# Row maxima of attention scores taken three rounds later, and their bf16 split moved inside GpSimd's turn

## The chip, the cores and the metric

The kernel runs on one core of one Trainium2 chip. The metric is the device time of one execution in microseconds (us), the median over several executions. It covers one transformer layer for 32 sequences of 256 tokens with 128 features.

## What is computed

The reference, cut to what matters:

```python
qkv = x @ W_qkv.T + b_qkv                      # x: (32, 256, 128), 16 heads of size 8
att = einsum('bthd,bshd->bhts', q, k) / sqrt(8)
att_v = einsum('bhts,bshd->bthd', softmax(att), v)
x = layernorm(x + att_v @ W_out.T + b_out)
# mixture of experts, 8 experts of 128 x 128, the 2 best per token, and one shared expert
x = layernorm(x + moe(x))
```

The change concerns the softmax only: exp(score - maximum of the row) is computed by putting the negated row maxima into the score matmul as two more rows of its contraction (a high and a low bf16 part), so the maxima of a batch must be known before its scores are exponentiated.

## The kernel before, in words

The engines are TensorE (PE in the profile), VectorE (DVE), ScalarE (ACT), GpSimd (POOL) and SyncE (SP, which issues DMAs). Each has its own instruction list, written out by hand, and waits on semaphores. Each list is in order.

The kernel has two stages. **Attention** takes the first 438 us or so, **the experts** the rest (groups of 512 tokens, lines 883 and 1141). The attention stage is a software pipeline over the 32 sequences, called batches. One step of the pipeline is a **turn** (a `Slot`, line 186, run from s = -4 to 31 by `slots`, line 207). In turn s each engine works on several batches at once:

- `proj`, batch s+4: q and k projections (PE L777 and L794), copied out by ACT (L616, L624), split into three bf16 parts by POOL (L466 to L495) and sent to HBM by SP (L355, L362)
- `stack`, batch s+3: SP reads the parts back as stacks of rows (L330), PE makes v (L790)
- `maxi`, batch s+2: PE computes plain scores into PSUM (`row_maxima_scores`, L699), DVE reduces each to row maxima (L1014)
- `neg`, batch s+1: POOL splits the negated maxima into two bf16 parts (L444, L446), PE transposes them (L826), DVE copies them out (L1055), SP writes them into the q stack (L336)
- `soft`, batch s: PE computes shifted scores (`shifted_scores`, L686), ACT takes exp (L561), PE multiplies by v (L714)
- `tail`, `norm`, `gated` (batches s-1, s-2, s-3): normalization of the attention result (PE L810, L848; DVE L1048, L1064), output projection (PE L770), residual (`x_bo`, POOL L460; `res`, DVE L1026) and layernorm (DVE L1029 to L1036; POOL `rstd` L473 and `x1_new` L482; PE transpose L842), transposed copy kept by POOL (L433), gate logits (PE L817)

PE's turn has eight **rounds** p = 0 to 7 of two heads each, that is 16 **steps**, one head per step. For a step PE issues, alternately, two matmuls L686 of batch s and two matmuls L699 of batch s+2; they use different halves of the rows of the array (`other = 1 - h % 2`, line 697) and overlap. Between rounds stand the other matmuls: L770 and L777 after round 0, L790 and L794 after round 2 (`PE_VQ`), L810, L817 and L826 after round 4 (`PE_TOK`), L842 and L848 after round 6 (`PE_BACK`), and L714 after rounds 1, 3, 5 and 7.

DVE's turn has the 16 reductions L1014 in order of the steps, and between them: `res` (L1026) after step 1's, stats (L1029) after step 2's, aggregate and `var_eps` (L1032, L1036) after step 4's, and after step 9's the copies and products L1048, L1055, L1058, L1064. `res` waits for PE's L777 of the same turn (L1020), the group after step 9 waits for L826 (L1044). In turn 30 the first routing work of the expert stage (`biased_scores`, L961 to L963) stands on DVE ahead of step 5.

**The banks.** Three PSUM banks hold scores for the maxima. PE may write a step's scores only when DVE has reduced the step that used the bank before:

```python
if i == 0 and (b.later(1) or h >= MAX_BACK[h]):
    pe.wait_ge(max_red, b.count(H, h + 1 - MAX_BACK[h]))
```

`three_banks(twice)` (line 157) gives the bank of each of the 16 heads and, as `MAX_BACK`, how many steps back the same bank was used. Sixteen heads don't divide by three, so one place of the order is irregular: banks run 0, 1, 2, 0, 1, 2, ... and at that place 0, 1, 2, 1. The distance is 3 everywhere but there, where it is 2, 4, 2, 4 for four heads in a row. ACT's banks (`EXP_BANK`) have the same rule with their own place.

Of the kernel before, what the change touches and what calls it, by code (L numbers as in the profile page):

```python
# [7 lines left out]
ALU = mybir.AluOpType  # L8
# [41 lines left out]
def attention_moe_layer(nc, x, xT, wqT, wkT, wvT, bq, bk, bv, woT, bo, gateT, ebias, rank, w1T, w3T, w2T, out):  # L50
# [3 lines left out]
    NT = T // P  # L54
    D = 8
    H = C // D
# [10 lines left out]
    PAIRS = H // 2  # L67
    assert C == P and H == 16 and NT == 2 and ROWS + 2 <= HALF

    with ExitStack() as ctx:  # L70
        def sb(name, shape, dt=F32):
            return ctx.enter_context(nc.sbuf_tensor(name, shape, dt))

        def sem(name):
            return ctx.enter_context(nc.semaphore(name))
# [20 lines left out]
        minus_half, ones = sb("minus_half", [P, GT]), sb("ones", [P, NT, 2, PAIRS])  # L96
# [10 lines left out]
        negmax = [sb(f"negmax{r}", [P, NT, H]) for r in range(2)]  # L107
# [3 lines left out]
        max_two = [sb(f"max_two{r}", [P, NT, 2, 2, PAIRS], BF16) for r in range(2)]  # L111
# [13 lines left out]
        max_ps, score_ps, av_ps, misc = banks[0:3], banks[3:6], banks[6], banks[7]  # L125
# [18 lines left out]
        v_set = sem("v_set")  # L144
        max_mm, max_red = sem("max_mm"), sem("max_red")
        max_hi_set, max_lo_set, max_T, max_rows_set = sem("max_hi_set"), sem("max_lo_set"), sem("max_T"), sem("max_rows_set")
# [10 lines left out]
        def three_banks(twice):  # L157

            order = [0, 1, 2] * (twice // 3) + [0, 1, 2, 1] + [0, 1, 2] * (4 - twice // 3)
            return order, [next(d for d in range(1, H) if order[(h - d) % H] == order[h]) for h in range(H)]  # L160

        MAX_BANK, MAX_BACK = three_banks(3)
        EXP_BANK, EXP_BACK = three_banks(9)


# [19 lines left out]

        class Slot:
            def __init__(self, i, s):
                self.load, self.proj, self.stack, self.maxi, self.neg, self.soft, self.tail, self.norm, self.gated = (
                    Batch(i, s + k, B) for k in (5, 4, 3, 2, 1, 0, -1, -2, -3))

        PE_YK, PE_VQ, PE_TOK, PE_BACK = 0, 2, 4, 6
        DVE_RES, DVE_STATS, DVE_AGGR, DVE_TOK = 1, 2, 4, 9
        ACT_K, ACT_ATT, ACT_V, ACT_Q, ACT_ATTC, ACT_X1T = 2, 4, 5, 6, 13, 14
# [209 lines left out]
        def _(pool):  # L405
# [27 lines left out]
                    pool.tensor_copy(x1T[:, bass.ds(b.n * T, T)], x1T_new[:]).then_inc(x1T_kept, 1)  # L433

            def rows_and_parts(t):
                b = t.neg
                if b.live:

                    negated = negmax[b.ring % 2][:].rearrange("p i (u g) -> p i u g", u=2)
                    two = max_two[b.ring % 2]  # L440
                    pool.wait_ge(max_red, b.count(H, H))
                    if b.later(2):
                        pool.wait_ge(max_T, b.count(1, -1))
                    pool.tensor_tensor(two[:, :, :, 0, :], negated, ones[:], ALU.mult).then_inc(max_hi_set, 1)  # L444
                    pool.wait_ge(max_hi_set, b.count(1, 1))
                    pool.tensor_tensor(two[:, :, :, 1, :], negated, two[:, :, :, 0, :], ALU.subtract).then_inc(max_lo_set, 1)  # L446
                p, o = t.proj, t.tail
                k_split, q_split = k_parts[p.ring % 2], q_parts[p.ring % 2]
                if o.live:
# [19 lines left out]
                b = t.norm  # L469
# [7 lines left out]
                        pool.wait_ge(x1_kept, b.count(16, 0))  # L477
                if p.live:
                    pool.tensor_tensor(k_split[:, 1, :], kf[:], k_split[:, 0, :], ALU.subtract).then_inc(split_step, 1)
                if b.live:  # L480
                    for i in range(NT):
                        pool.tensor_scalar(x1_new[:, i, :], res[:, i, :], mv[:, i, 0:1], rstd[:, i:i + 1],  # L482
                                           ALU.subtract, ALU.mult).then_inc(x1_set, 1)
# [194 lines left out]
        def _(pe):  # L678
# [12 lines left out]
            def row_maxima_scores(b, h, i):  # L691

                if i == 0 and h == 0:
                    pe.wait_ge(stack_in[b.ring], b.lap(64, 64))
                if i == 0 and (b.later(1) or h >= MAX_BACK[h]):
                    pe.wait_ge(max_red, b.count(H, h + 1 - MAX_BACK[h]))
                other = 1 - h % 2
                first, last = HALF * other, HALF * other + ROWS
                mm = pe.matmul(max_ps[MAX_BANK[h]][:, i * T:(i + 1) * T], q_stack[b.ring][first:last, h // 2, i * P:(i + 1) * P],  # L699
                               k_stack[b.ring][first:last, h // 2, :], start=True, stop=True)  # L700
                if i == NT - 1:
                    mm.then_inc(max_mm, 1)
# [37 lines left out]
            def slot(t, first=0, last=PAIRS):  # L740
                for p in range(first, last):
                    if (t.soft.c, p) == (B - 1, PE_ROUTED):
                        pe.wait_ge(max_red, H * B)
                        routing_by_tile(max_ps[2], 0, CHUNKS - 1, 1)
                    for h in (2 * p, 2 * p + 1):
                        for n in range(NT):
                            if t.soft.live:
                                shifted_scores(t.soft, h, n)
                            if t.maxi.live:
                                row_maxima_scores(t.maxi, h, n)  # L750

                    b = t.norm
                    if p == PE_YK and (b.live or t.proj.live):

                        if b.live:
                            pe.wait_ge(attc_set, b.count(1, 1))
                        elif t.soft.live:
                            pe.wait_ge(max_rows_set, t.soft.count(1, 1))
                        if t.gated.live:
                            pe.wait_ge(x1T_set, t.gated.count(1, 1))  # L760
                        if not b.live and t.proj.later(1):
                            pe.wait_ge(qk_f, t.proj.count(2, 0))
                            if t.proj.later(2):
                                pe.wait_ge(v_set, t.maxi.count(2, 2))
                    if b.live and p == PE_YK:

                        if b.c == 0:
# [4 lines left out]
                    b = t.proj  # L772
# [11 lines left out]
                    b = t.stack  # L784
# [7 lines left out]
                    b = t.proj  # L792
# [10 lines left out]
                    b = t.tail  # L803
# [8 lines left out]
                    b = t.gated  # L812
# [6 lines left out]
                    b = t.neg  # L819
# [17 lines left out]
                    b = t.norm  # L837
# [6 lines left out]
                    b = t.tail  # L844
# [66 lines left out]
        def _(dve):  # L911
# [26 lines left out]
            step = [0]  # L938
# [50 lines left out]
            def slot(t, first=0, last=H):  # L989
                for h in range(first, last):  # L990
# [14 lines left out]
                        dve.wait_ge(res_set, t.norm.count(1, 1))  # L1005
                    if t.norm.live and h == DVE_AGGR:
                        dve.wait_ge(stats_set, t.norm.count(NT, NT))
                    b = t.maxi
                    if b.live:
                        dve.wait_ge(max_mm, b.count(H, h + 1))  # L1010
                        if h == 0 and b.later(2):
                            dve.wait_ge(max_lo_set, b.count(1, -1))
                        column = PAIRS * (1 - h % 2) + h // 2
                        nc.vector.tensor_reduce(negmax[b.ring % 2][:, :, column], max_ps[MAX_BANK[h]][:].rearrange("p (i s) -> p i s", i=NT),  # L1014
                                                AX_X, ALU.max, negate=True).then_inc(max_red, 1)
                    b = t.norm
                    if b.live and h == DVE_RES:
# [27 lines left out]
                    b = t.tail  # L1045
# [3 lines left out]
                    b = t.neg  # L1049
# [6 lines left out]
                    b = t.gated  # L1056
                    if b.live and h == DVE_TOK:
                        nc.vector.tensor_copy(logits[:, bass.ds(b.n * NT, NT), :], gate_ps).then_inc(logits_set, 1)  # L1058
                    b = t.tail
# [166 lines left out]
```

## Time and profile before

| what | us |
|---|---|
| median of 3 runs | 787.43 (787.11 to 788.23) |
| the profiled execution, its own time | 788.83 |
| its span, from first to last instruction | 786.7 |
| PE busy | 750.0 (95% of the span) |
| DVE busy | 645.2 (82%) |
| ACT busy | 512.5 (65%) |
| POOL busy | 479.0 (61%) |

All times of the trace are counted from the start of the span. The busy time of an engine is an average over two stages with different limits: over the expert stage DVE is busy about two thirds of the time, in the attention stage nearly always. The attention stage must therefore be read by itself. A matmul's record lasts longer than the time until the next one starts, since matmuls are pipelined.

### The profile page before, as it was taken

How to read it: one execution, taken by the hardware profiler on the slowest of the kernel's cores; microseconds unless marked ns; L12 is line 12 of the kernel's file. 1: busy time of each engine (PE TensorE's matmuls, PEld its weight loads, DVE VectorE, ACT ScalarE, POOL GpSimd, SP SyncE). 2: the span in 40 equal slices, each digit the busy share in tenths (PEclk: the TensorE clock that was granted, in tenths of full speed). 3: DMA queues.
4: the chain of work that ended last, by engine and by line, in shares of the span. 5: the costliest groups of instructions: out<-in, count | busy, mean ns of one | idle time of the engine just before them, and what ended most of it. 6: DMA issues, size and time to landing. Idle time of an engine off the chain costs nothing.

```text
span 786.7 us, 20507 instructions
## 1 busy us (share of the span) xinstructions
PE 750.0 (95%) x6948; PEld 525.1 (67%) x6948; DVE 645.2 (82%) x1386; ACT 512.5 (65%) x1037; POOL 479.0 (61%) x653
## 2 busy tenths in 40 slices
PE   2889999999999999999999999899999999999995
PEld 1345555555555555555554688788888888888885
DVE  7689899999999999999998547976776666666665
ACT  1158788888888888888889645445545444554542
POOL 4345587876767667676634465565565566555554
PEclk9999999999999999999999999999999999999998
DMA  4646766566656665565531654454555545565440
GB/s 116 174 116 165 213 175 182 147 164 178 153 158 163 173 170 154 157 162 166 151 82 36 180 127 106 104 144 123 130 124 129 129 129 127 124 131 124 121 97 27
DMA packets 201449, 108.84 MB, mean 138 GB/s; under 512 B 10392, under 2 KB 200984, under 8 KB 201368
## 3 DMA queue, kind: packets, MB, share of 16 engines
q1 hardware_dynamic: 200048, 105.88, 52.1%
q10 hardware_dynamic: 1320, 1.91, 1.1%
q8 instruction: 47, 0.77, 0.5%
q14 instruction: 34, 0.28, 0.1%
HBM read 73.41 MB, written 33.82 MB: 136 GB/s over the span
## 4 chain that ended last, share of the span: by engine, by line
PE 86%; DVE 6%; DMA 3%; issue 2%; SPq 2%; ACT 1%; POOL 0%; POOLq 0%; DVEq 0%; ACTq 0%
PE bank L879 15%; PE bank L714 15%; PE bank L686 10%; PE bank L721 8%; PE bank L722 8%; PE bank L723 8%; PE bank L699 7%; PE bank L790 2%; PE bank L770 2%; PE bank L810 2%; DVE negmax L1014 2%; PE bank L777 2%; PE bank L794 2%; PE bank L817 1%; DMA q_stack<-max_rows 1%
## 5 line engine op out<-in xcount | busy, mean ns | idle before, releaser
L1014 DVE TENSOR_REDUCE negmax<-bank 128x2 f32<-128x512 f32 x512 | 320.1, 679 | 15.2 <-PE bank L699 12.8
L561 ACT ACTIVATE probs<-bank 128x512 f32<-128x512 f32 x512 | 291.8, 606 | 60.8 <-PE bank L686 57.0
L665 ACT ACTIVATE q_stack<-k_stack 128x512 f32<-128x512 f32 x128 | 80.8, 631 | 154.9 <-DVE k_stack L1077 154.9
L699 PE MATMUL bank<-k_stack,q_stack 48*128 48x256 bf16 x1024 | 162.7, 282 | 13.9 <-DMA k_stack<-k_parts_dram 9.8
L686 PE MATMUL bank<-q_stack,k_stack 50*128 50x256 bf16 x1024 | 156.2, 274 | 4.2 <-DMA q_stack<-max_rows 2.1
L1077 DVE TENSOR_TENSOR k_stack<-bank,probs 128x512 f32<-128x512 f32 x128 | 88.3, 690 | 74.8 <-PE bank L723 74.4
L714 PE MATMUL bank<-probs,v_aug 128*32 128x256 f32 x2048 | 137.1, 385 | 0.4 <-ACT attT L572 0.4
L686 PEld LDWEIGHTS bank<-q_stack,k_stack 50*128 50x128 bf16 x1024 | 75.2, 95 | 87.6 <-ACT probs L561 44.4
L721 PE MATMUL bank<-x_hi,hi_w 128*128 128x512 f32 x288 | 126.5, 439 | 3.1 <-DVE k_stack L1087 1.2
L722 PE MATMUL bank<-x_hi,lo_w 128*128 128x512 f32 x288 | 114.0, 396 | 0.0
L723 PE MATMUL bank<-x_lo,hi_w 128*128 128x512 f32 x288 | 113.6, 394 | 0.0
L514 POOL TENSOR_TENSOR k_stack<-k_stack,probs 128x512 f32<-128x512 f32 x48 | 62.0, 1291 | 50.9 <-DVE k_stack L1087 42.2
L699 PEld LDWEIGHTS bank<-k_stack,q_stack 48*128 48x128 bf16 x1024 | 71.4, 96 | 32.0 <-issue 14.3
L879 PEld LDWEIGHTS bank<-w_sb,k_stack 128*128 128x128 f32 x640 | 83.4, 191 | 7.1
L714 PEld LDWEIGHTS bank<-probs,v_aug 128*32 128x32 f32 x2048 | 53.6, 109 | 49.2 <-issue 15.2
L879 PE MATMUL bank<-w_sb,k_stack 128*128 128x128 f32 x640 | 84.0, 274 | 0.0
L514 POOL TENSOR_TENSOR place<-k_stack,probs 128x512 f32<-128x512 f32 x48 | 61.9, 1290 | 30.4 <-PE bank L879 25.6
L649 ACT ACTIVATE probs<-probs 128x512 f32<-128x512 f32 x128 | 78.9, 616 | 0.4 <-DMA probs<-route_dram 0.4
L514 POOL TENSOR_TENSOR k_stack<-q_stack,probs 128x512 f32<-128x512 f32 x32 | 41.1, 1284 | 53.0 <-DVE q_stack L1087 44.1
L1087 DVE TENSOR_TENSOR k_stack<-bank,q_stack 128x512 f32<-128x512 f32 x96 | 65.6, 683 | 4.1 <-POOL k_stack L514 3.6
L723 PEld LDWEIGHTS bank<-x_lo,hi_w 128*128 128x128 f32 x288 | 54.1, 188 | 13.4
L721 PEld LDWEIGHTS bank<-x_hi,hi_w 128*128 128x128 f32 x288 | 54.5, 189 | 11.4 <-DVE k_stack L1087 1.6
(103 smaller groups left out, 1111.3 us busy)
## 6 DMA issues: line engine op xcount, KB each, us to landing
probs<-route_dram SPq DMA_DIRECT2D x128, 256.0 KB, 4.9
q_stack<-q_parts_dram SPq DMA_DIRECT2D x64, 192.0 KB, 3.3
k_stack<-k_parts_dram SPq DMA_DIRECT2D x64, 192.0 KB, 4.1
k_parts_dram<-k_parts SPq DMA_DIRECT2D x32, 192.0 KB, 2.2
q_parts_dram<-q_parts SPq DMA_DIRECT2D x32, 192.0 KB, 2.1
xT_sb<-xT SPq DMA_DIRECT2D x32, 128.0 KB, 2.3
k_parts_dram<-k_parts SPq DMA_DIRECT2D x32, 128.0 KB, 2.0
q_parts_dram<-q_parts SPq DMA_DIRECT2D x32, 128.0 KB, 1.9
```

Of the source, the lines that this page charges most:

```text
L514: pool.tensor_tensor(hid_s[n % DEPTH], hid[n % DEPTH], weight2_b[n - 1], ALU.mult).then_inc(hids_set, 1)
L561: nc.scalar.activation(probs[h][:], score_ps[EXP_BANK[h]][:].rearrange("p (j t) -> p j t", j=NT), ACT.Exp).then_inc(exp_done, 1)
L665: nc.scalar.activation(act[n % DEPTH], gated[n % DEPTH] if n else up1_ps[0][:], ACT.Silu).then_inc(act_set, 1)
L686: mm = pe.matmul(score_ps[EXP_BANK[h]][:, j * T:(j + 1) * T], k_stack[b.ring][first:last, h // 2, j * P:(j + 1) * P], q_stack[b.ring][firs ...
L699: mm = pe.matmul(max_ps[MAX_BANK[h]][:, i * T:(i + 1) * T], q_stack[b.ring][first:last, h // 2, i * P:(i + 1) * P], k_stack[b.ring][first: ...
L714: mm = pe.matmul(av_ps[32 * hh:32 * hh + 32, half * T:(half + 1) * T], v_aug[b.ring][:, 2 * j + half, u, hh, :], probs[4 * quad + hh][:, j ...
L721: pe.matmul(ps[:], w_hi[m][:, n, :], hi[:], start=start, stop=False)
L722: pe.matmul(ps[:], w_lo[m][:, n, :], hi[:], start=False, stop=False)
L723: return pe.matmul(ps[:], w_hi[m][:, n, :], lo[:], start=False, stop=stop)
L879: mm = pe.matmul(down_ps[r][:, i * P:(i + 1) * P], (hid_s if n else hid)[n % DEPTH][:, i * P:(i + 1) * P], w2_sb[:, n, :], start=(n == 0 a ...
L1014: nc.vector.tensor_reduce(negmax[b.ring % 2][:, :, column], max_ps[MAX_BANK[h]][:].rearrange("p (i s) -> p i s", i=NT), AX_X, ALU.max, neg ...
L1077: nc.vector.tensor_tensor(gated[n % DEPTH], up1_ps[n % DEPTH][:], weight_b[e], ALU.mult).then_inc(gated_set, 1)
```

## The change

It has four parts:

1. A turn's 16 steps of maxima no longer belong to one batch. Steps 0 to 5 work on heads 10 to 15 of batch s+1 (`neg`), steps 6 to 15 on heads 0 to 9 of batch s+2 (`next`, the new name of `maxi`). This holds on PE and on DVE alike. `maxima(step)` gives batch and head.
2. The bank order of the maxima is `three_banks(12)` in place of `three_banks(3)`. Banks go with heads, not with steps.
3. POOL's split of the maxima (L444, L446) moves from the start of its turn to behind the second k part (L479), ahead of `x1_new` (L482). It still waits until all 16 heads of the batch are reduced (in the block marked "..." ahead of `b = t.norm` stand the removed lines, unchanged).
4. The wait of L764 and DVE's waits name the new objects; the counts follow from batch and head.

Nothing else moves: the number of instructions of every kind, the transposes, the copies and the DMAs of the maxima keep their places in the turn.

```diff
-        MAX_BANK, MAX_BACK = three_banks(3)
+        MAX_BANK, MAX_BACK = three_banks(12)
...
-                self.load, self.proj, self.stack, self.maxi, self.neg, self.soft, ...
+                self.load, self.proj, self.stack, self.next, self.neg, self.soft, ...
+            def maxima(self, step):
+                return (self.neg, step + H - MAX_FROM) if step < MAX_FROM else (self.next, step - MAX_FROM)
+        MAX_FROM = 6
...
             def rows_and_parts(t):
-                b = t.neg
-                if b.live:
-                    negated = negmax[b.ring % 2][:].rearrange("p i (u g) -> p i u g", u=2)
-                    two = max_two[b.ring % 2]
-                    pool.wait_ge(max_red, b.count(H, H))
-                    if b.later(2):
-                        pool.wait_ge(max_T, b.count(1, -1))
-                    pool.tensor_tensor(two[:, :, :, 0, :], negated, ones[:], ALU.mult).then_inc(max_hi_set, 1)
-                    pool.wait_ge(max_hi_set, b.count(1, 1))
-                    pool.tensor_tensor(two[:, :, :, 1, :], negated, two[:, :, :, 0, :], ALU.subtract).then_inc(max_lo_set, 1)
...
                 if p.live:
                     pool.tensor_tensor(k_split[:, 1, :], kf[:], k_split[:, 0, :], ALU.subtract).then_inc(split_step, 1)
+                b = t.neg
+                if b.live:
...
+                b = t.norm
                 if b.live:
                     for i in range(NT):
                         pool.tensor_scalar(x1_new[:, i, :], res[:, i, :], mv[:, i, 0:1], rstd[:, i:i + 1],
...
                     for h in (2 * p, 2 * p + 1):
+                        ahead, head = t.maxima(h)
                         for n in range(NT):
                             if t.soft.live:
                                 shifted_scores(t.soft, h, n)
-                            if t.maxi.live:
-                                row_maxima_scores(t.maxi, h, n)
+                            if ahead.live:
+                                row_maxima_scores(ahead, head, n)
...
-                                pe.wait_ge(v_set, t.maxi.count(2, 2))
+                                pe.wait_ge(v_set, t.next.count(2, 2))
...
-                    b = t.maxi
+                    b, head = t.maxima(h)
                     if b.live:
-                        dve.wait_ge(max_mm, b.count(H, h + 1))
-                        if h == 0 and b.later(2):
+                        dve.wait_ge(max_mm, b.count(H, head + 1))
+                        if head == 0 and b.later(2):
                             dve.wait_ge(max_lo_set, b.count(1, -1))
-                        column = PAIRS * (1 - h % 2) + h // 2
-                        nc.vector.tensor_reduce(negmax[b.ring % 2][:, :, column], max_ps[MAX_BANK[h]][:].rearrange("p (i s) -> p i s", i=NT),
+                        column = PAIRS * (1 - head % 2) + head // 2
+                        nc.vector.tensor_reduce(negmax[b.ring % 2][:, :, column], max_ps[MAX_BANK[head]][:].rearrange("p (i s) -> p i s", i=NT),
                                                 AX_X, ALU.max, negate=True).then_inc(max_red, 1)
```

## Rows read from the trace of the kernel before

**Rows 1.** The page's costliest group: the reductions (busy, mean ns; idle before, releaser)

```profile
L1014 DVE TENSOR_REDUCE negmax<-bank 128x2 f32<-128x512 f32 x512 | 320.1, 679 | 15.2 <-PE bank L699 12.8
```

**Rows 2.** Busy time by stretch (stretch, length, PE, PEld, DVE, ACT, POOL, PEclk, DMA share, GB/s)

```profile
120.00:243.00 123.00, 122.85 (x1536) 70.97 (x1536) 120.10 (x260) 106.75 (x235) 89.32 (x155) 1.00 0.62 163
243.00:366.00 123.00, 123.00 (x1544) 71.06 (x1540) 120.22 (x261) 105.74 (x231) 85.58 (x150) 1.00 0.61 163
```

**Rows 3.** Waits between 60 and 440 us (us in total, times, longest us)

```profile
DVE negmax L1014 <- PE bank L699: 3.1, 6, 1.8
...
PEld bank L699 <- DVE negmax L1014: 1.9, 3, 1.3
```

**Rows 4.** Timeline of DVE, turn 16 (start us, us, engine line op, xcount)

```profile
245.30 0.42 DVE L1026 TENSOR_TENSOR res<-bank,x_bo 128x256 f32<-128x256 f32 x1
...
246.76 1.27 DVE L1014 TENSOR_REDUCE negmax<-bank 128x2 f32<-128x512 f32 x2
...
248.57 3.09 DVE L1014 TENSOR_REDUCE negmax<-bank 128x2 f32<-128x512 f32 x5
251.80 0.36 DVE L1048 RECIPROCAL recip_sum<-bank 128x32 f32<-128x32 f32 x1
...
252.62 5.00 DVE L1014 TENSOR_REDUCE negmax<-bank 128x2 f32<-128x512 f32 x8
257.60 0.42 DVE L1026 TENSOR_TENSOR res<-bank,x_bo 128x256 f32<-128x256 f32 x1
```

**Rows 5.** Timeline of PE, the same turn

```profile
244.66 0.60 PE L777 MATMUL bank<-xT_sb,wk_sb 128*128 128x256 f32 x2
...
246.86 0.38 PE L699 MATMUL bank<-k_stack,q_stack 48*128 48x256 bf16 x2
...
248.48 0.38 PE L699 MATMUL bank<-k_stack,q_stack 48*128 48x256 bf16 x2
...
251.38 0.29 PE L826 MATMUL bank<-ident_bf,max_two 128*32 128x128 bf16 x2
...
253.69 0.44 PE L842 MATMUL bank<-ident,x_new 128*128 128x128 f32 x2
...
256.96 0.60 PE L777 MATMUL bank<-xT_sb,wk_sb 128*128 128x256 f32 x2
```

**Rows 6.** Timeline of POOL, the same turn and the start of the next

```profile
249.53 0.68 POOL L479 TENSOR_TENSOR k_parts<-kf,k_parts 128x256 bf16<-128x256 f32 x1
...
256.69 0.25 POOL L446 TENSOR_TENSOR max_two<-negmax,max_two 128x32 bf16<-128x32 f32 x1
```

**Rows 7.** Timeline of PE, then of DVE, turn 29, rounds 2 and 3

```profile
406.20 0.37 PE L686 MATMUL bank<-q_stack,k_stack 50*128 50x256 bf16 x2
407.57 0.28 PE L699 MATMUL bank<-k_stack,q_stack 48*128 48x256 bf16 x1 [0.99 <-DVE negmax L1014]
...
406.24 1.27 DVE L1014 TENSOR_REDUCE negmax<-bank 128x2 f32<-128x512 f32 x2
```

**Rows 8.** Timeline of DVE, turn 30

```profile
416.16 0.43 DVE L1026 TENSOR_TENSOR res<-bank,x_bo 128x256 f32<-128x256 f32 x1 [0.66 <-PE bank L770]
...
417.93 2.55 DVE L962 RECIPROCAL q_stack<-q_stack 128x384 f32<-128x384 f32 x1
...
421.82 0.36 DVE L1048 RECIPROCAL recip_sum<-bank 128x32 f32<-128x32 f32 x1 [0.75 <-PE bank L826]
```

**Rows 9.** Timeline of DVE, then of PE, turns -2 to 0

```profile
21.94 1.29 DVE L1014 TENSOR_REDUCE negmax<-bank 128x2 f32<-128x512 f32 x2 [3.58 <-PE bank L699]
...
27.51 7.47 DVE L1014 TENSOR_REDUCE negmax<-bank 128x2 f32<-128x512 f32 x12 [1.45 <-PE bank L699]
...
39.51 2.68 DVE L1014 TENSOR_REDUCE negmax<-bank 128x2 f32<-128x512 f32 x4 [1.45 <-PE bank L699]
42.10 0.27 DVE L1055 COPY max_rows<-bank 32x256 bf16<-32x256 bf16 x1
...
45.20 0.39 PE L686 MATMUL bank<-q_stack,k_stack 50*128 50x256 bf16 x1 [0.37 <-DMA q_stack<-max_rows]
```

More of the change, by code:

```diff
@@ L187, in __init__ @@
             def __init__(self, i, s):
-                self.load, self.proj, self.stack, self.maxi, self.neg, self.soft, self.tail, self.norm, self.gated = (
+                self.load, self.proj, self.stack, self.next, self.neg, self.soft, self.tail, self.norm, self.gated = (
                     Batch(i, s + k, B) for k in (5, 4, 3, 2, 1, 0, -1, -2, -3))
+            def maxima(self, step):
+                return (self.neg, step + H - MAX_FROM) if step < MAX_FROM else (self.next, step - MAX_FROM)
+        MAX_FROM = 6
         PE_YK, PE_VQ, PE_TOK, PE_BACK = 0, 2, 4, 6
@@ L479, in rows_and_parts @@
                     pool.tensor_tensor(k_split[:, 1, :], kf[:], k_split[:, 0, :], ALU.subtract).then_inc(split_step, 1)
+                b = t.neg
+                if b.live:
+                    negated = negmax[b.ring % 2][:].rearrange("p i (u g) -> p i u g", u=2)
+                    two = max_two[b.ring % 2]
+                    pool.wait_ge(max_red, b.count(H, H))
+                    if b.later(2):
+                        pool.wait_ge(max_T, b.count(1, -1))
+                    pool.tensor_tensor(two[:, :, :, 0, :], negated, ones[:], ALU.mult).then_inc(max_hi_set, 1)
+                    pool.wait_ge(max_hi_set, b.count(1, 1))
+                    pool.tensor_tensor(two[:, :, :, 1, :], negated, two[:, :, :, 0, :], ALU.subtract).then_inc(max_lo_set, 1)
+                b = t.norm
                 if b.live:
```

## The prediction

> **What bounds the kernel now.** The busy shares of the whole span mix two stages, so I read the attention stage by stretch first. Between 120 and 366 us PE is busy in 245.85 of 246 us and DVE in 240.3, that is 12.0 us of each 12.3 us turn; ACT with 212.5 us and POOL with 174.9 have room [rows 2]. PE is the bound and DVE stands 0.3 us per turn behind it. The waits say the same: from 60 to 440 us PE's weight loads waited for a reduction three times, 1.9 us together, and DVE waited for score matmuls six times, 3.1 us [rows 3]. The three banks between the two engines work almost without a stall.
>
> Then the timeline of turn 16, engine by engine. PE's L777 starts at 244.66 and again at 256.96: a turn is 12.30 us [rows 5]. DVE is tied to PE at two places. `res` starts at 245.30, just after L777 ends at 244.66 + 0.60 = 245.26; the reciprocal after step 9 starts at 251.80, 0.13 after L826 ends at 251.67 [rows 4, 5]. From the reciprocal to the next `res` DVE needs 5.80 us without a gap, PE from the end of L826 to the end of L777 5.89. So neither half of the turn has more than some 0.2 us to give, and what holds PE up in the first half moves L826, DVE's reciprocal and everything behind them.
>
> **The change part by part.** *Same work.* In a full turn PE issues 64 score matmuls and DVE 16 reductions, as before. The parity of head and step stays equal, so the two kinds of score matmul still use different halves of the array. This costs nothing, since no instruction is added.
>
> *The bank order.* Worked out from line 157: before, the distance is 2 for heads 6 and 8 (steps 6 and 8) and 4 for 7 and 9. Now it is 2 for heads 15 and 1, 4 for heads 0 and 2. Those heads are at steps 5 and 7 (distance 2) and 6 and 8 (distance 4). So step 5's scores wait for step 3's reduction, where they waited for step 2's, and step 7's for step 5's. Step 6 was the first step after L790 and L794 and step 8 the first after an L714 block, where DVE had had time; step 5 is the second step of its round, and ahead of it DVE has done `res` and the stats.
>
> - Step 5: the pair of L699 at 246.86 lasts 0.38, so the second, step 5's first, starts at 246.86 + 0.11 = 246.97 [rows 5]. DVE does steps 3 and 4 from 246.76 [rows 4]; one reduction is 0.68 [rows 1], so step 3 ends at 247.44. How fast PE follows is to be seen in turn 29: DVE's pair ends at 406.24 + 1.27 = 407.51, PE's step 6 goes at 407.57 after 0.99 us of idle time [rows 7]. With that 0.06, step 5 goes at 247.50: 0.53 us late.
> - Step 7: its first matmul is at 248.48 + 0.11 = 248.59 [rows 5], now at 249.12. DVE's step 5 starts at 248.57 [rows 4] (its scores are there in time, by 247.9) and ends at 249.25; step 7 goes at 249.31, another 0.19 us late.
>
> Together 0.72 us. L826 ends at 252.39, the reciprocal starts at 252.52, the next L777 ends at 258.28 where it ended at 257.56: a turn of 13.02 us. DVE can't win it back, for `res` stays tied to L777 and step 3's reduction to `res`; the 2.14 us from `res` to the end of step 3 are DVE work without a gap. The turns with `res` and 16 steps of maxima are 2 to 29. Turns 28 and 29 lack projections, but already wait for DVE there (0.99 us in turn 29 [rows 7]), so I give them the same price. 28 x 0.72 = 20.2 us. From both sides: 0.53 if the second wait is swallowed, 0.9 if ACT or the weight loads add to it: 14.8 to 25.2 us.
>
> *The split on POOL.* Both operations last 0.25, 0.6 us with the hand-over [rows 6]. Now they follow L479, which ends at 250.21 [rows 6]; step 5's reduction is done at 249.25, so POOL doesn't wait, and the split is ready at 250.8. L826 starts at 251.38 and by the above at 252.1: 0.6 us of cover, soon 1.3. `x1_new` (1.6 us) comes 0.6 later, at 252.4, and L842 needs it at 253.69 [rows 5], by then 254.4: covered too. Behind it the k and q parts leave POOL 0.6 later; SP sends them in its own order, behind the maxima's DMAs, and they are read only a turn later. Cost 0; if the cover were gone, each 0.1 us late would cost 0.1 us per turn.
>
> *The start.* Turn -2 had 16 reductions and has 10, so 26 instead of 32 stand before turn 0. Its projections stood between maxima, behind the wait for the first stack; now they are issued before that wait. Before: reductions from 21.94, 26 of them before the copy at 42.10, with holes of 1.45 us at 27.51 and 39.51 behind L790 and L794, first shifted scores at 45.20, 3.1 us behind the copy [rows 9]. Now 20 reductions at 0.62 (the eight at 252.62 take 5.00 [rows 4]) are 12.4, with the holes of turn -1 alone, some 2.3: copy at 36.7, scores at 39.8. Gain 5.4 us; between 3.7 (six reductions alone) and 6.5.
>
> *The end.* Turn 30 gets the six steps that turn -2 lost. On DVE two reductions (1.24) stand ahead of `res`, which had 0.66 idle before it: +0.6. Then steps 2 to 4, and only then the routing block (its reciprocal alone 2.55 [rows 8]), step 5's reduction, POOL's split and L826. Between `res` at 416.16 and the reciprocal at 421.82 DVE works 4.9 us of 5.66; with four reductions (2.5), split (0.6) and L826 (0.4) that is 8.4. So L826 and all behind it come 0.6 + 8.4 - 5.66 = 3.3 us later; between 2 and 4.5.
>
> Sum: 20.2 + 3.3 - 5.4 = +18.1 us. The profiled execution took 788.83, 1.4 above the median of 787.43; against its own time that is 806.9, against the median **805.5**.
>
> **The rivals.** *The bank waits cost the turn nothing (faster).* PE's records last longer than its work, and DVE's 12.0 us could be the true bound. Then PE would wait at steps 5 and 7 where it otherwise waits elsewhere, and only start and end would count: 3.3 - 5.4 = -2.1, 785.3 us. It decides if PE has over 0.7 us of slack between step 7 and L826. For it: turn 29 had a wait of 0.99 without being a long turn [rows 7]. Against it: that turn has no L777, L790 and L794, and in turn 16 DVE's reciprocal waits for L826, not the reverse [rows 4, 5].
>
> *The split comes too late.* POOL stands behind `kf`, `rstd` and L479, and if it falls over 1.3 us behind, L826 waits for it. At half a microsecond in each of 28 turns this adds 14 us to the forecast: 819 us. The cover computed above speaks against it.
>
> *TensorE's clock falls.* Turn 0's first score matmul lasts 0.39 us, later ones 0.28 [rows 7, 9]; the granted clock is 1.00 between 120 and 366 us [rows 2]. If short waits let it fall to the lower of its two levels in one turn in ten, three turns would last up to twice as long, +37 us over the forecast: 842 us. Against it, the matmul right after the wait of 0.99 us still lasts 0.28 [rows 7]. The Trainium skill, "TensorE: Matmul & The Clock Gate", section "A second HAM failure mode: psum-queue depth-cycling", speaks against this change: cycling through PSUM banks with small idle gaps between groups of matmuls made the clock swing between its levels. By that rule the new waits would bring this rival's time; by rows 7 they bring their own length only, and I go by the rows.
>
> *The start gains nothing.* If turn -1 waits at step 6 for the second stack, the 5.4 us shrink; with all of it gone 811 us. That the bank order isn't what I read can't be: it follows from one line.
>
> **How the numbers follow.** Forecast 0.80, waits that cost nothing 0.10, late split 0.05, clock 0.02, the start without gain 0.03. The range takes the bounds of the forecast: low 14.8 + 2 - 6.5 = +10.3, high 25.2 + 4.5 - 3.7 = +26, so 797.7 to 813.4, rounded outward to 797 to 815 for the terms not seen; the start without gain is inside, the other rivals outside. A measurement of this kernel can tell about 0.2% (1.6 us) from no change. Faster by more than that: the first rival and little else, 0.10; within: 0.03; slower: 0.87.
>
> **What would show it.** In the profile after, a full turn (L777 to L777) should last 13.0 us; PE should wait for L1014 about 0.5 us in round 2 and 0.2 in round 3 of each turn, some 20 us in all where it was 1.9; DVE should wait some 0.5 us per turn for L699 or L826. The first L686 should stand near 39.8, turn 30's reciprocal some 8.4 us behind its `res`. Turns of 12.3 us, or waits of PE for reductions under 5 us in all, would prove the main step wrong; waits of L826 for POOL would prove the second rival.

## The result and the profile after

The changed kernel takes 808.55 us (808.36 to 810.45), the kernel before, on the same chip, 787.56 us: 1.0264 times as long, with a 95% interval of 1.0240 to 1.0288, or 21.0 us more. The forecast was 805.5, inside a range of 797 to 815. The profiled execution took 808.6 us with a span of 806.4, that is 19.7 us more than the span of before.

The two stretches that took 123 us each, with PE full, are no longer full. Windows of the profile after, in the columns of [rows 2]:

```profile
120.00:250.00 130.00, 127.52 (x1544) 71.07 (x1540) 121.87 (x261) 108.58 (x235) 88.80 (x154) 1.00 0.57 154
250.00:380.00 130.00, 127.52 (x1542) 71.12 (x1540) 121.90 (x260) 107.44 (x231) 84.88 (x150) 1.00 0.58 154
```

The same number of matmuls (1544) now takes 130 us instead of 123, and the granted clock is 1.00. PE's busy time is up too, by 4.5 us: a score matmul's record lasts 0.28 us while the next may start 0.11 us behind it, so a short wait is half hidden under the record before it. The busy share alone would show only 2.5 us of idle time where PE lost 7. Where the time goes is seen in the waits between 60 and 450 us and in the page's costliest group (compare [rows 3] and [rows 1]):

```profile
PEld bank L705 <- DVE negmax L1021: 22.8, 57, 1.1
...
DVE negmax L1021 <- PE bank L705: 13.1, 29, 0.6
PE bank L705 <- DVE negmax L1021: 9.1, 30, 0.8
...
PE bank L833 <- POOL max_two L484: 3.1, 1, 3.1
```

```profile
L1021 DVE TENSOR_REDUCE negmax<-bank 128x2 f32<-128x512 f32 x512 | 324.6, 680 | 29.0 <-PE bank L705 23.7
```

PE's weight loads for the maxima scores now wait for a reduction 57 times, 22.8 us together, where [rows 3] had three waits and 1.9 us: two waits in each full turn. (The matmul's own line shows only 9.1 us, since its idle time is counted from the end of the record before.) DVE in turn waits 29 times, once a turn. Each engine waits for the other, and neither is full.

One turn, PE first (the timeline of the profile after; start us, us, engine line op, xcount):

```profile
248.88 0.60 PE L784 MATMUL bank<-xT_sb,wk_sb 128*128 128x256 f32 x2
...
251.07 0.27 PE L705 MATMUL bank<-k_stack,q_stack 48*128 48x256 bf16 x1
251.18 0.27 PE L692 MATMUL bank<-q_stack,k_stack 50*128 50x256 bf16 x1
251.70 0.28 PE L705 MATMUL bank<-k_stack,q_stack 48*128 48x256 bf16 x1 [0.25 <-DVE negmax L1021]
...
253.33 0.27 PE L692 MATMUL bank<-q_stack,k_stack 50*128 50x256 bf16 x1
253.51 0.28 PE L705 MATMUL bank<-k_stack,q_stack 48*128 48x256 bf16 x1
...
256.31 0.28 PE L833 MATMUL bank<-ident_bf,max_two 128*32 128x128 bf16 x2
...
258.62 0.44 PE L849 MATMUL bank<-ident,x_new 128*128 128x128 f32 x2
```

and DVE in the same turn:

```profile
249.51 0.42 DVE L1033 TENSOR_TENSOR res<-bank,x_bo 128x256 f32<-128x256 f32 x1
...
250.97 1.27 DVE L1021 TENSOR_REDUCE negmax<-bank 128x2 f32<-128x512 f32 x2
...
255.29 1.29 DVE L1021 TENSOR_REDUCE negmax<-bank 128x2 f32<-128x512 f32 x2 [0.44 <-PE bank L705]
256.73 0.36 DVE L1055 RECIPROCAL recip_sum<-bank 128x32 f32<-128x32 f32 x1
...
262.52 0.42 DVE L1033 TENSOR_TENSOR res<-bank,x_bo 128x256 f32<-128x256 f32 x1
```

Step 5's first score matmul could have gone at 251.18, beside the L692 there. DVE's pair of reductions from 250.97 holds step 3's, which ends at 250.97 + 0.68 = 251.65, and the matmul goes at 251.70: 0.52 us late. Step 7's goes at 253.51, 0.18 behind the L692 at 253.33. That is 0.70 us, and a turn from `res` to `res` lasts 262.52 - 249.51 = 13.01 us, where it was 12.30. The reciprocal again stands just behind L833 (256.73 against 256.31 + 0.28), and from it to the next `res` are 5.79 us, as before: what PE lost in the first half is not won back in the second.

### The profile page after: what moved, and what is told of

It reads as the page before. It is cut to its first block, busy times and chain, and to the rows that moved or that the text cites. A ratio compares the mean times of both kernels' runs of the same rounds, so it can differ in the third digit from the quotient of the medians.

```text
span 806.4 us, 20509 instructions
## 1 busy us (share of the span) xinstructions
PE 765.8 (95%) x6948; PEld 526.5 (65%) x6948; DVE 648.9 (80%) x1386; ACT 518.1 (64%) x1037; POOL 477.0 (59%) x653
## 3 DMA queue, kind: packets, MB, share of 16 engines
q1 hardware_dynamic: 200048, 105.88, 51.1%
## 4 chain that ended last, share of the span: by engine, by line
PE 77%; DVE 16%; issue 3%; DMA 2%; ACT 1%; POOL 0%; SPq 0%; POOLq 0%; DVEq 0%; ACTq 0%
PE bank L886 15%; PE bank L720 12%; DVE negmax L1021 9%; PE bank L692 9%; PE bank L727 8%; PE bank L728 8%; PE bank L729 8%; PE bank L705 7%; PE bank L797 3%; PE bank L817 2%; PE bank L801 2%; DVE res L1033 2%; DVE stats L1036 1%; PE bank L849 1%; PE bank L824 1%
## 5 line engine op out<-in xcount | busy, mean ns | idle before, releaser
L1021 DVE TENSOR_REDUCE negmax<-bank 128x2 f32<-128x512 f32 x512 | 324.6, 680 | 29.0 <-PE bank L705 23.7
L705 PE MATMUL bank<-k_stack,q_stack 48*128 48x256 bf16 x1024 | 173.7, 282 | 12.6 <-DVE negmax L1021 11.4
L692 PE MATMUL bank<-q_stack,k_stack 50*128 50x256 bf16 x1024 | 164.4, 277 | 1.6 <-ACT probs L567 1.0
L720 PE MATMUL bank<-probs,v_aug 128*32 128x256 f32 x2048 | 139.5, 391 | 0.2 <-ACT attT L578 0.2
L692 PEld LDWEIGHTS bank<-q_stack,k_stack 50*128 50x128 bf16 x1024 | 75.4, 95 | 86.3 <-ACT probs L567 42.0
L705 PEld LDWEIGHTS bank<-k_stack,q_stack 48*128 48x128 bf16 x1024 | 68.1, 96 | 41.2 <-DVE negmax L1021 32.2
L720 PEld LDWEIGHTS bank<-probs,v_aug 128*32 128x32 f32 x2048 | 54.0, 110 | 50.5 <-issue 21.8
L454 POOL TENSOR_TENSOR x_bo<-x_sb,bo_sb 128x256 f32<-128x256 f32 x32 | 23.1, 723 | 88.5 <-ACT kf L622 61.1
```

Of the source, the lines that this page charges most:

```text
L692: mm = pe.matmul(score_ps[EXP_BANK[h]][:, j * T:(j + 1) * T], k_stack[b.ring][first:last, h // 2, j * P:(j + 1) * P], q_stack[b.ring][firs ...
L720: mm = pe.matmul(av_ps[32 * hh:32 * hh + 32, half * T:(half + 1) * T], v_aug[b.ring][:, 2 * j + half, u, hh, :], probs[4 * quad + hh][:, j ...
```

## The experiments

**The bank order alone, put back.** The shift by three rounds and the split stay as changed; only the place of the doubled entry in the order of banks goes to 9, which puts the two short distances at steps 2 and 4.

```
-        MAX_BANK, MAX_BACK = three_banks(12)
+        MAX_BANK, MAX_BACK = three_banks(9)
```

> The changed kernel with one argument altered: the bank order of the maxima has its two distances of 2 at heads 12 and 14, that is at steps 2 and 4. Theory (the whole loss per turn is the two bank waits at steps 5 and 7): step 2 needs the reduction of step 0, step 4 that of step 2, and both are over before PE comes there (before: step 0's reduction ended at about 244.7, step 2's scores went at 245.19; step 2's ended at 246.44, step 4's scores went at 246.74). So turns of 12.30 us, no waits of L705 for reductions in a full turn, 808.5 - 28 x 0.71 = 788.6 us, up to 790.5 if the wait of turn 4 for the maxima's DMA (about 2 us before, none after) comes back with the shorter turns. Rival (spreading a batch's maxima over two turns, or the place of the split on GpSimd, lengthens the turn by itself): turns over 12.6 us and a time over 797 us.

Measured: 786.51 us (785.34 to 787.89), 0.9982 of before, interval 0.9972 to 0.9992. Two L784 in the timeline of PE:

```profile
238.21 0.60 PE L784 MATMUL bank<-xT_sb,wk_sb 128*128 128x256 f32 x2
...
250.51 0.60 PE L784 MATMUL bank<-xT_sb,wk_sb 128*128 128x256 f32 x2
```

The turn is 12.30 us again. The bank order alone costs 808.55 - 786.51 = 22.0 us, slightly more than the whole loss. Neither the shift nor the split costs anything in a full turn. The wait of turn 4 (below) did not come back, and the time is still 2.1 us under the 788.6 that were expected for that case. In the traces, 20.4 instead of 19.9 us lie between `res` of turn 2 and of turn 30 (the last two of these turns lost 0.9 us each, not 0.71), 0.6 at the start and 0.4 in turn 30; the rest is the difference between the profiled executions and the medians.

**The bank order alone, in the kernel before.** The reverse test: nothing is shifted, no split is moved, only the order of banks is turned by one place.

```
-        def three_banks(twice):
+        def three_banks(twice, turn=0):
             order = [0, 1, 2] * (twice // 3) + [0, 1, 2, 1] + [0, 1, 2] * (4 - twice // 3)
+            order = order[turn:] + order[:turn]
...
-        MAX_BANK, MAX_BACK = three_banks(3)
+        MAX_BANK, MAX_BACK = three_banks(3, 1)
```

> The kernel before with its bank order turned by one place, so that the distances of 2 stand at steps 5 and 7 and nothing else differs. Theory: the same two waits as after the change, 0.54 and 0.18 us per turn in turns 2 to 29, 12.30 becomes 13.0 us: 787.5 + 20 = 807.5 us (805 to 809), without the changes at the start and in turn 30. Rival (the waits come from the new distribution of the heads over turns): 787.5 us.

Measured: 809.53 us (808.93 to 809.66), 1.0275, interval 1.0258 to 1.0292, a little over the top of what was expected. `res` of turns 3 to 5 stands at 85.92, 98.94 and 111.96: 13.02 us a turn. The rule on distances therefore holds in either kernel, and the loss needs nothing of the rest of the change. The part over the expectation is at the start, where `res` of turn 2 comes at 73.22 instead of 71.20: slow score matmuls last until about 54.6 us, not 51.1. Why the start is longer here was not tried. The wait of turn 4 for a DMA (below) is gone in this run too, 2.0 us the other way.

**A bank order between the two.** With the doubled entry at 0 the short distances lie at steps 9 and 11, where DVE still has some lag from `res` and the stats.

```
-        MAX_BANK, MAX_BACK = three_banks(12)
+        MAX_BANK, MAX_BACK = three_banks(0)
```

> The changed kernel with the bank order's distances of 2 at heads 3 and 5, that is at steps 9 and 11. Theory (a wait is the end of the reduction two steps before, plus 0.06, less the time at which TensorE comes there): in the turn of the kernel before, step 7's reduction ends at 248.57 + 2 x 0.60 + 0.68 = 250.45 and step 9's scores went at 250.14, so 0.37 us; step 9's reduction ends at 251.66 and step 11's scores went at 251.83, so nothing. Turns of 12.67 us, 786.5 + 28 x 0.37 = 796.9 us (795 to 799). Rival (any irregular place that comes behind another instruction of VectorE costs the same): 808 us; or none but the place of steps 5 and 7 costs anything: 786.5 us.

Measured: 797.30 us (797.21 to 797.43), 1.0101, interval 1.0062 to 1.0141. The timeline of DVE:

```profile
247.98 3.10 DVE L1021 TENSOR_REDUCE negmax<-bank 128x2 f32<-128x512 f32 x5
251.58 0.36 DVE L1055 RECIPROCAL recip_sum<-bank 128x32 f32<-128x32 f32 x1 [0.51 <-PE bank L833]
```

The turns are 12.67 us (`res` at 92.68, 105.34, 118.01). Step 9's scores go 0.36 us late, at 249.91, before L833, and that is what a turn pays. Step 11's short distance lies behind L833 and costs nothing. So the same method met three sizes: 0.72, 0.37 and 0 us a turn.

**The split back at the start of POOL's turn.** Everything else as changed. It tests the cover that the prediction gave the split, from the other side.

```
             def rows_and_parts(t):
+                b = t.neg
+                if b.live:
...
+                    pool.tensor_tensor(two[:, :, :, 1, :], negated, two[:, :, :, 0, :], ALU.subtract).then_inc(max_lo_set, 1)
                 p, o = t.proj, t.tail
```

> The changed kernel with GpSimd's split of the maxima back at the start of its turn. It then holds x_bo, the k parts, rstd and x1_new until step 5's reduction is over. Worked out from the changed kernel's turn with res at 249.51: step 5's reduction ends at 253.46, then 0.6 + 0.7 + 0.4 + 0.7 + 0.7 + 0.7 + 1.6 us of GpSimd work, x1_new done at about 258.9, where TensorE wants it at 258.62: some 0.3 to 0.5 us per turn, 808.5 + 10 = 818 us (814 to 824). Rival (GpSimd has room enough, the place of the split is free): 808.5 us.

Measured: 811.50 us (809.21 to 812.75), 1.0290, interval 1.0268 to 1.0312: only some 3 us over the changed kernel, so the expectation was wrong. The wait itself is there, in waits and in the timelines of POOL, PE (L849), DVE and PE (L705):

```profile
POOL max_two L449 <- DVE negmax L1021: 125.6, 29, 8.7
...
PE bank L849 <- POOL x_new L488: 7.4, 26, 0.6
```

```profile
255.30 0.25 POOL L449 TENSOR_TENSOR max_two<-negmax,ones 128x32 bf16<-128x32 f32 x1 [4.28 <-DVE negmax L1021]
```

```profile
260.80 0.41 PE L849 MATMUL bank<-ident,x_new 128*128 128x128 f32 x2 [0.28 <-POOL x_new L488]
```

```profile
254.46 0.17 DVE L1043 TENSOR_SCALAR var_eps<-mv 128x2 f32<-128x2 f32 x1
```

```profile
255.25 0.38 PE L705 MATMUL bank<-k_stack,q_stack 48*128 48x256 bf16 x2
```

POOL stands 4.28 us in front of its turn, and L849 waits for `x_new` some 0.28 us a turn. But the turn grew by only 0.09 us, to 13.10 (L784 at 250.90 and 264.00). DVE's way from `res` to the reciprocal is shorter by 0.19: 251.54 to 258.57 is 7.03, in the changed kernel 249.51 to 256.73 is 7.22. The row of `var_eps` tells why: with POOL idle beside it, it lasts 0.17 us, in the changed kernel 0.43 (medians of all 32: 169 against 429 ns). It stands just ahead of step 5's reduction, and on that reduction hangs PE's second bank wait. Step 7's scores now go 0.11 us behind step 6's (the pair at 255.25), without the 0.18 us of the changed kernel. So 0.28 us lost at L849 stand against some 0.19 won at step 7, and the turn grows by the difference.

In the trace the 27 turns cost 2.2 us. Another 1.5 came in turn 29, which lasted 14.20 us from its `res` to the next against 12.69. There PE waited 0.61 and 0.83 us for reductions, and the granted clock fell behind the second wait (windows, in the columns of [rows 2]):

```profile
421.50:425.00 3.50, 2.06 (x31) 0.92 (x24) 3.43 (x11) 3.04 (x7) 0.01 (x1) 1.00 0.00 0
425.00:428.40 3.40, 3.40 (x28) 1.21 (x29) 1.59 (x3) 1.23 (x3) 3.22 (x6) 0.51 0.02 5
```

The changed kernel has the same two waits in its turn 29, at 419.89 and 421.22, and keeps 1.00.

**The move of the split alone.** The changed kernel with the maxima back at their old place and the old bank order.

```
-        MAX_BANK, MAX_BACK = three_banks(12)
+        MAX_BANK, MAX_BACK = three_banks(3)
...
-        MAX_FROM = 6
+        MAX_FROM = 0
```

> The changed kernel with MAX_FROM = 0 and the bank order of before: all 16 maxima of a batch in one turn, as before, and of the change only the place of GpSimd's split in the middle of its turn. Theory (the split is ready 0.6 us ahead of L826 and x1_new 1.3 us ahead of L842 there, so the move alone is covered): turns of 12.30 us and 787.5 us (786.5 to 788.5). Rival (the later x1_new or k parts cost something, as the DMAs of the parts are late for turn 4): 789 us or more.

Measured: 787.83 us (786.98 to 793.11), 0.9984, interval 0.9960 to 1.0008. It costs nothing that can be measured.

**The routing scores one step later.** In turn 30 the routing block stands between step 4's and step 5's reduction. Here it begins behind step 5's.

```
-        DVE_SCORES, DVE_FIRST, DVE_SECOND, DVE_WEIGHTS, DVE_ROUTED = (-2, 5), (-2, 10), (-1, 5), (-1, 6), (-1, 13)
+        DVE_SCORES, DVE_FIRST, DVE_SECOND, DVE_WEIGHTS, DVE_ROUTED = (-2, 6), (-2, 10), (-1, 5), (-1, 6), (-1, 13)
```

> The changed kernel with the routing block of turn 30 on VectorE one step later, behind step 5's reduction in place of ahead of it. Theory (turn 30 loses 3.1 us to TensorE's wait for the split, and 2.5 us more since the granted clock falls to 0.53 after that wait): the wait for the split goes, matmuls of round 5 last 0.28 instead of 0.39, VectorE's reciprocal comes some 7.5 us behind res (8.7 after, 5.7 before) and holds round 6 about 1 us: 808.5 - 4.7 = 803.8 us (802.5 to 805). Rival (the 2.5 us are not the clock but work behind the split): only the wait comes back, 805.5 us or more, with the intervals behind the split as long as after.

Measured: 804.52 us (803.63 to 805.94), 1.0214, interval 1.0193 to 1.0235, 4.0 us under the changed kernel. First turn 30 of the changed kernel, the timelines of PE and DVE and one window in the columns of [rows 2]:

```profile
435.55 0.51 PE L824 MATMUL bank<-gate_sb,x1T_new 128*128 128x8 f32 x4
439.18 0.39 PE L833 MATMUL bank<-ident_bf,max_two 128*32 128x128 bf16 x2 [3.11 <-POOL max_two L484]
...
440.04 1.93 PE L720 MATMUL bank<-probs,v_aug 128*32 128x256 f32 x16
```

```profile
431.01 0.41 DVE L1033 TENSOR_TENSOR res<-bank,x_bo 128x256 f32<-128x256 f32 x1
...
437.60 0.69 DVE L1021 TENSOR_REDUCE negmax<-bank 128x2 f32<-128x512 f32 x1
439.71 0.36 DVE L1055 RECIPROCAL recip_sum<-bank 128x32 f32<-128x32 f32 x1 [1.41 <-PE bank L833]
...
446.92 0.42 DVE L1033 TENSOR_TENSOR res<-bank,x_bo 128x256 f32<-128x256 f32 x1 [3.50 <-PE bank L777]
```

```profile
439.10:446.00 6.90, 6.82 (x54) 2.54 (x54) 3.58 (x9) 4.47 (x9) 2.37 (x5) 0.53 0.20 59
```

PE waits 3.11 us for the split, and behind the wait the granted clock is 0.53, near the lower of its two levels (1.2 GHz): a block of 16 L720 lasts 1.93 us, in a full turn 1.07. From the reciprocal to the next `res` it is 7.21 us, before 4.68 (421.82 to 426.50). Now the same places with the routing block one step later, PE and then DVE:

```profile
435.98 0.29 PE L833 MATMUL bank<-ident_bf,max_two 128*32 128x128 bf16 x2
...
436.52 1.07 PE L720 MATMUL bank<-probs,v_aug 128*32 128x256 f32 x16
...
439.10 0.44 PE L849 MATMUL bank<-ident,x_new 128*128 128x128 f32 x2 [1.18 <-DVE att_tok L1071]
```

```profile
438.15 0.36 DVE L1055 RECIPROCAL recip_sum<-bank 128x32 f32<-128x32 f32 x1
...
442.38 0.42 DVE L1033 TENSOR_TENSOR res<-bank,x_bo 128x256 f32<-128x256 f32 x1 [0.49 <-PE bank L777]
```

L833 doesn't wait, L720 keeps its 1.07 us, PE waits 1.18 us elsewhere and the clock holds. The reciprocal is 1.56 us earlier and the next `res` 4.54: 1.56 were the wait, the other 2.98 are what followed on it. That this is the clock above all is borne out by the run with `three_banks(0)`: its turn 30 has the same wait (3.12 us), but the clock is at the lower level for 3.4 us instead of 6.8, and from the reciprocal to the next `res` it is 5.96 us, between the 7.21 and the 4.23 here.

**Both repairs.** The changed kernel with `three_banks(9)` and the routing scores one step later.

> The changed kernel with both repairs: bank order 9 (as in e1) and the routing block one step later (as in e4). Theory (the two losses are independent, 22.0 us and 4.0 us): 786.5 - 4.0 = 782.5 us (781 to 784), faster than the kernel before by 0.65%. Rival (with the shorter turns the wait for the split or another wait returns in turn 30): 785 us or more.

Measured: 782.49 us (782.05 to 783.17), 0.9913, interval 0.9884 to 0.9942. It beats both kernels, the changed one by 26.1 us, the one before by 5.5 (its median beside these runs was 787.99). This is what the shift is worth when its two side effects are taken away, if the later routing scores alone bring the kernel before nothing; that was not run.

**The clock at the start.** Matmuls at the start last 0.39 us instead of 0.28. Useless matmuls were added to the kernel with both repairs (128 columns, bf16, into a score bank that is written again before it is read; nothing else changes) to keep PE at work: 36 in front of turn -2, 8 behind its projections, and 4 behind each step of maxima in turns -2 and -1.

```
+            def warm(count):
+                for _ in range(count):
+                    pe.matmul(score_ps[0][:, 0:P], ident_bf[:], ident_bf[:], start=True, stop=True)
...
+                        if ahead.live and not t.soft.live:
+                            warm(4)
...
+                            warm(8)
```

> e5 with matmuls of no use (128 columns, bf16, into a score bank that turn 0 overwrites) ahead of and between TensorE's work of turns -2 and -1: 36 while it would wait for xT, 8 ahead of the first stack, 4 per step of maxima. Theory (in turn 0 matmuls take twice their time for 9.3 us since TensorE's clock is at the lower level; L784 of turn 1 comes 14.1 us after that of turn 0, where 12.0 lie between the next two): matmuls of turn 0 last 0.28 instead of 0.39, that distance falls to some 12, 780 us (779 to 781.5). Rival (turn 0 is long for the filling of the pipeline, not for the clock): 782.5 us, or more since the added matmuls delay the maxima.

Measured: the runs of this kernel fall apart, four of ten near 780 (779.9 to 780.2), four near 795 (794.7 to 795.9), two between; the median of all ten is 785.51, which is not what was expected. The ratio of the six under 790 is 0.9909 (0.9876 to 0.9942). The mean granted clock of the four near 780 is 0.996 to 0.997, of the four near 795 it is 0.972 to 0.974. The profiled execution, 794.68, is one of the long ones (timeline of PE, then windows in the columns of [rows 2]):

```profile
20.93 0.39 PE L705 MATMUL bank<-k_stack,q_stack 48*128 48x256 bf16 x2 [2.27 <-DMA k_stack<-k_parts_dram]
```

```profile
20.90:28.00 7.10, 7.07 (x43) 3.26 (x44) 4.63 (x7) 0.00 (x0) 1.37 (x3) 0.56 0.64 182
...
34.00:50.00 16.00, 16.00 (x85) 7.41 (x85) 8.60 (x14) 1.29 (x4) 5.16 (x10) 0.50 0.23 60
...
60.00:70.00 10.00, 9.45 (x124) 4.92 (x122) 8.84 (x15) 8.34 (x17) 4.50 (x9) 1.00 0.36 109
```

PE waited 2.27 us for the first stack, the clock fell, and it stayed at the lower level while PE was busy in 16.00 of 16 us. At that level the useless matmuls are themselves in the way: a step takes 1.08 us and holds DVE up.

**The gap filled.** The same with 44 matmuls where there were 8, so that PE works until the first stack is there.

```
-                            warm(8)
+                            warm(44)
```

> e6 with 44 instead of 8 added matmuls ahead of the first stack. e6 ran in two ways: 779.9 us, or about 795 us with the granted clock at 0.50 from 21 to 55 us. Theory (in its profile the clock falls right after TensorE's wait of 2.27 us for the first stack, and at the lower level the added matmuls hold up the maxima, 1.08 us per step instead of 0.62): with the wait filled the clock stays, nearly all executions take 779.9 us (779 to 781), so e6's good case always. Rival (the clock falls for another reason, in which the amount of work in the steps of maxima has a part): again both cases, a spread of over 5 us, medians of 783 us or more.

Measured: 780.48 us (779.58 to 786.91; five of six under 781.5), 0.9898, interval 0.9855 to 0.9940. Windows:

```profile
20.90:38.00 17.10, 16.99 (x151) 8.99 (x152) 15.15 (x24) 1.28 (x4) 6.57 (x13) 1.00 0.67 181
38.00:50.00 12.00, 10.93 (x135) 5.94 (x138) 11.40 (x20) 9.18 (x20) 5.13 (x10) 1.00 0.59 158
```

The wait before the first stack is 0.29 us, the clock stays, and `res` of turn 2 comes at 63.68 instead of 66.76 in the kernel with both repairs. Of these 3.1 us the span keeps 2.8 (781.0 to 778.2). Against the kernel before beside each, the medians give 2.0 us (787.99 - 782.49 and 788.02 - 780.48), and the intervals of the two ratios overlap. So the low clock at the start costs some 2 to 3 us in the kernel with both repairs, by this estimate. None of the six runs is near 795, but one is at 786.91 with a mean clock of 0.992. With four long runs of ten before, six without one, on another chip, make it likely, not certain, that the wait of 2.27 us was what brought the clock down.

## Why the prediction was right, and where it was not

The forecast's mechanism held: 18.1 us were expected and 21.0 measured, and the bank order alone brings 22.0. Span against span (19.7), by the prediction's own steps; a kernel's `res` rows are the marks:

- **The bank waits: 20.2 forecast, 19.9 measured.** Step 5 was to be 0.53 us late and is 0.52, step 7 0.19 and is 0.18, the turn 13.02 and is 13.01. Putting the order back (12.30 us) and turning it in the kernel before (13.02 us) show that it is this cause, and the third order (12.67) that its size follows from the distance and the step.
- **The first rival (waits that cost the turn nothing)** fell: PE has no slack ahead of L833. Its time, 785.3, is near what the kernel with the old distances takes, which is as it should be, since without the bank waits only start and end count.
- **The split: 0 forecast, 0 measured.** L482 starts at 254.37, right behind L473, the split ends 254.94, and L833 at 256.31 doesn't wait. Moved alone it changes nothing. The rival of the late split does not occur in any full turn; in turn 30 alone, where its input is late, PE waits for it.
- **The start: a gain of 5.4 forecast, 3.6 measured at `res` of turn 2.** The first shifted scores came at 39.28, forecast 39.8, before 45.20: this step was right and the gain there is 5.9. But turn 0 then ran some 10 us with slow matmuls (from 39.28 to about 49.7), before some 6 (from 45.20 to about 51.1). An earlier turn 0 is a slower turn 0. The prediction had the row of 0.39 us and did not ask for how long it would last.
- **A term not in the sum: 2.0 us gained.** Before, L686 waited in turn 4 for the maxima's DMA:

```profile
95.41 0.28 PE L686 MATMUL bank<-q_stack,k_stack 50*128 50x256 bf16 x1 [1.59 <-DMA q_stack<-max_rows]
```

  The 2.0 us are what three turns there lasted over 12.30 us (14.03, 12.60 and 12.48 us up to `res` of turns 4, 6 and 9), less some 0.2 elsewhere. In the changed kernel the wait is gone. It is gone as well with the old bank order put back (turns of 12.30 us) and in the kernel before with its banks turned (13.02 us), and with the split moved alone, where turns -2 to 1 have their old work, the turns over 12.30 us (12.40, 12.72 and 12.48) add up to 0.7 us, not 2.2. So neither the longer turns nor the shorter start is needed to lose it. It was seen in one execution, which took 1.3 us more than the median of its kernel; how much of it the median holds, and what brings it about, stays open.
- **The end: 3.3 forecast, 6.2 measured up to `res` of turn 31.** This is the step that was mis-sized. `res` of turn 30 lost 0.6 us to its two reductions, and the reciprocal stands 8.70 us behind it, forecast 8.4, before 5.66: together 3.6. What the sum lacked is the fall of the clock behind the wait of 3.11 us, 2.5 us more from reciprocal to `res` (7.21 against 4.68). The prediction worked out an L833 that would be late, but not that PE would stand idle for all of that time, and it priced "TensorE's clock falls" for the short waits of the full turns only. Some 0.7 us of it come back by the end. With the routing scores one step later this addition is gone.

The sum: 19.9 - 3.6 - 2.0 + 6.2 - 0.7 = 19.8, against 19.7 between the spans. The start's 1.8 and the end's 2.9 made it longer than forecast, turn 4's 2.0 and the end's last 0.7 shorter; the large term was right. That the terms which were off cancel in part is luck. Between the medians it is 21.0, since the profiled execution of before was a long one for its kernel.

**TensorE's clock** thus fell in one place of the changed kernel's running pipeline, turn 30, where the rival had it fall in three turns. In the full turns each holds two waits, of 0.52 and 0.18 us, and the granted clock is 1.00 in both windows of 130 us above. The section "A second HAM failure mode: psum-queue depth-cycling" of the Trainium skill's page "TensorE: Matmul & The Clock Gate" has short idle gaps at a PSUM ring make the clock swing; the 57 such waits of this kernel don't bear it out. One place of another run does: with the split first, the lower level came for 3.4 us in turn 29 behind waits of 0.61 and 0.83 us, the longest there. The single waits of 3.11 and 2.27 us went with the lower level, those of 1.18 and (in turn 4 of before) 1.59 us did not. The length of the single wait alone therefore doesn't say what the clock will do.

## What to carry to other kernels

In a ring of buffers with unequal distances, where the short distances fall in the period matters as much as their number: for each step compare the end of the consumer's operation that many steps back with the time at which the producer arrives, and put the short ones where the consumer has just had time to catch up. If work is shifted against the rest, shift the ring's order with it. At the ends of a pipeline, ask of every late input how long TensorE stands idle before it: waits of the size of the 2.27 and 3.11 us here, and several shorter ones close together, have to be priced with the slower matmuls that may follow, and moving other work out of the way can be worth more than the wait itself (4.0 us here).

## What was not expected of the hardware

- The clock did not come back under a load of small matmuls: in the profile of the first warm start PE was busy for 16.00 of 16 us (34 to 50 us) at a granted 0.50, and the shifted scores of turn 0 still began slow, at 51.52; it was at 1.00 only from 60 us on. With the gap filled it read 1.00 from 20.9 to 50 us. The quick runs of the two kernels are equally quick (779.9 to 780.2 and 779.6 to 781.4).
- The granted clock at the very start is no evidence. In the changed kernel it reads 1.00 for turn 0's first 10 us, while the matmuls last up to twice as long as later ones (windows, in the columns of [rows 2]; timeline of PE):

```profile
39.00:49.60 10.60, 9.99 (x64) 4.74 (x64) 6.25 (x11) 5.57 (x13) 4.00 (x9) 1.00 0.62 160
```

```profile
40.24 1.22 PE L784 MATMUL bank<-xT_sb,wk_sb 128*128 128x256 f32 x2
...
54.80 0.70 PE L784 MATMUL bank<-xT_sb,wk_sb 128*128 128x256 f32 x2
```

  There the durations are to be read: L784 at 1.22 us where it is 0.70 a turn later.
- DVE's `var_eps`, two numbers in each partition, lasts 0.43 us beside a working POOL and 0.17 beside an idle one; in turn 30 of the changed kernel, where POOL is idle from 432.30 to 434.16, `var_eps` at 433.92 lasts 0.17 as well. When it is long, it ends just behind POOL's instruction (timelines of POOL and DVE, changed kernel, turn 16):

```profile
252.16 0.67 POOL L462 TENSOR_TENSOR rk<-kf,k_parts 128x256 f32<-128x256 f32 x1
```

```profile
252.43 0.43 DVE L1043 TENSOR_SCALAR var_eps<-mv 128x2 f32<-128x2 f32 x1
```

  It ends at 252.86, some 0.02 us behind L462, and so do all 26 long ones of the changed kernel (0.02 to 0.03 us behind their L462). The Trainium skill's page "SBUF — State Buffer", section "Who interferes with whom", has DVE and GpSimd share a pair of ports as a lock: when DVE's instruction is in one of its 2-port modes, whichever engine comes first keeps the pair for its whole instruction, and the other waits. The rows agree with such a lock. That `var_eps` runs in a 2-port mode was not shown.
